# First feed-forward block: slices run on across batches two apart, time mixing's sums, keys and running maximum one slice later

## The reference

```python
x = x + tanh(g_ffn[0]) * L0_ffn(layernorm(x))
#   up = x @ wu.T; gate = x @ wg.T; out = (silu(up) * gate) @ wd.T     wu, wg: 2048 x 512, ternary
x = x + tanh(g_xattn[1]) * L1_xattn(w, u, k=layernorm(x), v=ctx_2048)
#   time mixing, for t in 0..255, per channel, carrying (p, q, o):
#   no = max(o, u + k_t); A = exp(o - no); E = exp(u + k_t - no)
#   y_t = (A * p + E * v_t) / (A * q + E)
#   no2 = max(w + o, k_t); p, q = exp(w + o - no2) * (p, q) + exp(k_t - no2) * (v_t, 1)
```

## Time and profile before

| | us |
|---|---|
| median of three runs | 3331.32 (3331.31 to 3336.03) |
| profiled execution | 3330.52 |
| its span | 3328.7 |
| PE busy | 2915.2 (88%) |
| DVE busy | 2454.5 (74%) |
| ACT busy | 1777.8 (53%) |
| POOL busy | 939.5 (28%) |
| mean granted TensorE clock | 0.95 of full |

### The profile page before, as it was taken

How to read it: one execution, slowest core, us unless ns; L and a number is a source line. 1 busy time by engine, 2 the same in 40 slices (tenths; PEclk the granted TensorE clock), 3 DMA queues, 4 the chain that set the end, 5 groups by cost and what they waited for, 6 DMA issues and landing times.

```text
span 3328.7 us, 48608 instructions
## 1 busy us (share of the span) xinstructions
PE 2915.2 (88%) x18346; PEld 1700.8 (51%) x18346; DVE 2454.5 (74%) x4452; ACT 1777.8 (53%) x2803; POOL 939.5 (28%) x1409
## 2 busy tenths in 40 slices
PE   8999989883899898668888667999999999998999
PEld 4444766652444444456666433545455445443666
DVE  7887578887666666788888668777777777776433
ACT  3331455555455554089998964444454444445444
POOL 5543000002200000046776774222222222211000
PEclk9999999996899999889999878999999999999999
DMA  7422212212111011100000021000000000011000
GB/s 251 142 98 74 64 56 66 64 51 83 31 27 33 18 26 64 48 26 1 1 1 1 28 87 47 7 1 7 1 7 7 1 7 7 1 48 58 13 14 26
DMA packets 60422, 132.78 MB, mean 40 GB/s; under 512 B 6496, under 2 KB 27808, under 8 KB 59424
## 3 DMA queue, kind: packets, MB, share of 16 engines
q1 hardware_dynamic: 50976, 96.11, 9.3%
q10 hardware_dynamic: 9216, 33.56, 3.3%
HBM read 119.03 MB, written 4.19 MB: 37 GB/s over the span
## 4 chain that ended last, share of the span: by engine, by line
PE 46%; DVE 16%; ACT 9%; issue 4%; POOL 3%; DMA 0%; DVEq 0%; ACTq 0%; SPq 0%; POOLq 0%
PE psum L1289 10%; PE psum L2257 5%; PE psum L2787 4%; PE psum L3258 3%; PE psum L3236 3%; PE psum L2746 3%; ACT area_g L2332 3%; PE psum L2771 3%; PE psum L2138 2%; PE psum L2756 2%; PE psum L2278 2%; DVE area_a L1898 2%; PE psum L1544 2%; PE psum L1525 2%; ACT xn L2898 1%
## 5 line engine op out<-in xcount | busy, mean ns | idle before, releaser
L2332 ACT ACTIVATE area_g<-area_a 128x2048 bf16<-128x2048 f32 x168 | 334.6, 1995 | 31.6 <-POOL area_a L2201 22.4
L2257 PE MATMUL psum<-area_c,ident_bf 128*128 128x128 bf16 x3328 | 234.3, 236 | 94.1 <-DVE area_c L2366 94.0
L660 PE MATMUL psum<-area_b,area_g 128*128 128x512 f32 x640 | 280.9, 596 | 2.2 <-issue 2.2
L2257 PEld LDWEIGHTS psum<-area_c,ident_bf 128*128 128x128 bf16 x3328 | 219.0, 107 | 119.9 <-DVE area_c L2366 112.7
L2746 PE MATMUL psum<-area_b,stage 128*128 128x512 f32 (+1 forms) x512 | 237.5, 546 | 0.0
L848 PE MATMUL psum<-xT_high,area_a 128*128 128x256 f16 x1024 | 230.9, 276 | 4.4 <-DVE area_b L1095 2.9
L848 PE MATMUL psum<-xT_low,area_a 128*128 128x256 f16 x1024 | 230.5, 276 | 0.0
L2898 ACT ACTIVATE xn<-psum,small 128x384 f32<-128x384 f32 (+1 forms) x256 | 163.8, 640 | 96.0 <-DVE small L3037 95.8
L3037 DVE TENSOR_REDUCE small<-psum 128x1 f32<-128x384 f32 (+1 forms) x256 | 158.1, 618 | 71.5 <-PE psum L2747 69.0
L2663 POOL TENSOR_TENSOR small<-small,half_pow 128x4 f32<-128x4 f32 x96 | 131.8, 1373 | 273.6 <-DVE small L2984 273.6
L660 PEld LDWEIGHTS psum<-area_b,area_g 128*128 128x128 f32 x640 | 120.7, 191 | 148.2 <-issue 144.1
(11 more groups left out here) (426 smaller groups left out, 7388.7 us busy)
## 6 DMA issues: line engine op xcount, KB each, us to landing
stage<-in_w ACTq DMA_DIRECT2D x24, 512.0 KB, 4.5
stage<-in_w SPq DMA_DIRECT2D x24, 512.0 KB, 3.7
area_g<-in_toeplitz SPq DMA_DIRECT2D x32, 256.0 KB, 2.7
area_b<-in_ctxT SPq DMA_DIRECT2D x15, 512.0 KB, 4.1
area_b<-area_b SPq DMA_DIRECT2D x24, 256.0 KB, 3.7
stage<-in_ctxT SPq DMA_DIRECT2D x9, 512.0 KB, 3.8
x_stream<-in_x SPq DMA_DIRECT2D x4, 1024.0 KB, 8.0
area_c<-in_ctxT SPq DMA_DIRECT2D x8, 512.0 KB, 7.8
```

What stands on the lines that cost most here:

```text
L660: last = nc.tensor.matmul(psum[:, bank + m, :], toep[:, h % 2, (m - k) * P:(m - k + 1) * P], kv[:, h % 2, k, :], start=(k == 0), stop=(k = ...
L2257: last = nc.tensor.matmul(psum[:, 1, t_ * P:(t_ + 1) * P], identb[:, :], above5[:, t_, c * P:(c + 1) * P], start=(c == 0), stop=(c == KE - 1))
L2332: nc.scalar.activation(junk5[t_], z5[b % 3][:, t_, :], ACT.Sign, bias=fine5[:, par, t_:t_ + 1], scale=-1.0, accum_out=signs5[:, t_:t_ + 1] ...
```

## The change

TensorE: the last two downs of a batch move behind `up_gate` 0 and 1 of the next batch, so that `down` runs two slices behind `up_gate` throughout, and `y_back` of tile 0 goes with them; `keys` move from slices 2 and 3 to 3 and 4. ScalarE: `scaled` of time mixing moves from slice 0 to 1, `key_copy` from 2 and 3 to 3 and 4. VectorE: the addition to X becomes a function, `ffn0_add`, and goes from the end of the batch to slice 1 of the next one, behind L1115; time mixing's norm sums go from slice 0, ahead of L1115, to slice 1, behind `ffn0_add`; `running_max` goes from slice 4 to 5. The wait for `front_bank_free` is written inside the loop but stands where it stood. No instruction is added or dropped; POOL's and SP's orders stay.

```diff
@@ -866,9 +866,9 @@
             for t_ in range(TT):
                 transpose_front(pe, front_of_ffn(0), t_)
             for b in range(B):
-                f = front_of_ffn(b)
-                pe.wait_ge(sig("front_bank_free"), tile_no(f, TT))
                 for j in range(NJ):
+                    if j == 0:
+                        pe.wait_ge(sig("front_bank_free"), tile_no(front_of_ffn(b), TT))
                     if b == 0 and j < 2:
                         pe.wait_ge(sig("conv_added"), B + 3 + 2 * j)
                     if b == 0 and j == 2:
@@ -876,15 +876,19 @@
                     up_gate(b, j)
                     if j == 2:
                         y_back(b - 3, 1)
-                    if j in (2, 3):
-                        keys(b - 1, j - 2)
+                    if j in (3, 4):
+                        keys(b - 1, j - 3)
                     if j in (4, 6) and b + 1 < B:
                         transpose_front(pe, front_of_ffn(b + 1), j // 2 - 2)
                     if j >= 2:
                         down(b, j - 2)
-                down(b, NJ - 2)
-                y_back(b - 2, 0)
-                down(b, NJ - 1)
+                    elif b:
+                        down(b - 1, NJ - 2 + j)
+                    if j == 0:
+                        y_back(b - 3, 0)
+            down(B - 1, NJ - 2)
+            y_back(B - 3, 0)
+            down(B - 1, NJ - 1)
             keys(B - 1, 0)
             y_back(B - 3, 1)
             keys(B - 1, 1)
@@ -956,12 +960,12 @@
                                          ACT.Copy, scale=2.0 ** -26).then_inc(sig("hid_high_ready"), 1)
                     if j == 0:
                         present_exp(b - 2)
-                    if j == 0 and b:
+                    if j == 1 and b:
                         scaled(act, front_of_wkv(b - 1), b - 1)
                     if j == 3 and b + 1 < B:
                         scaled(act, front_of_ffn(b + 1), b + 1)
-                    if j in (2, 3):
-                        key_copy(b - 1, j - 2)
+                    if j in (3, 4):
+                        key_copy(b - 1, j - 3)
                     if j in (1, 2, 3, 5, 6):
                         sum_later(act, 5 * b + (1, 2, 3, 5, 6).index(j))
                     if j in (4, 6) and b + 1 < B:
@@ -1085,6 +1089,13 @@
                     nc.vector.tensor_tensor_scan(wk_p[:, k, 1:S + 1], wk_d[:, 2, k, :], wk_ev[:, k, :], 0.0,
                                                  ALU.mult, ALU.add).then_inc(sig("wkv_pq_ready"), 1)
 
+            def ffn0_add(b):
+                for t_ in range(TT):
+                    xt = X[:, b * TT + t_, :]
+                    dve.wait_ge(sig("down_ready"), b * TT + t_ + 1)
+                    nc.vector.scalar_tensor_tensor(out=xt, in0=psum[:, 6 + t_, :], scalar=S1("ffn0"), in1=xt,
+                                                   op0=ALU.mult, op1=ALU.add).then_inc(sig("ffn0_added"), 1)
+
             for b in range(B):
                 for j in range(NJ):
                     n = b * NJ + j
@@ -1094,16 +1105,13 @@
                                                            in1=psum[:, 2 + 2 * (j % 2), :], op0=ALU.add, op1=ALU.mult))
                     nc.vector.tensor_tensor(hid[:, j % 2, :], act_a[:, j % 2, :], psum[:, 3 + 2 * (j % 2), :],
                                             ALU.mult).then_inc(sig("hid_ready"), 1)
-                    if j == 0 and b:
-                        dve.wait_ge(sig("ffn0_added"), TT * b + TT)
-                        norm_sums(dve, dc, front_of_wkv(b - 1), b - 1)
                     if j == 1:
                         products(b - 2)
                     if j == 2:
                         totals(b - 2)
                     if j == 3:
                         invert(b - 2, 0)
-                    if j == 4:
+                    if j == 5:
                         running_max(b - 1)
                     if j in (5, 7) and b + 1 < B:
                         ffn_low(dve, (b + 1) * TT + (j - 5) // 2 + 1, (b + 1) % 2, (j - 5) // 2)
@@ -1116,6 +1124,10 @@
                                                    in0=hid[:, j % 2, :].rearrange("p (m s) -> p m s", m=2),
                                                    scalar=2.0 ** -26, in1=hTh[:, 2 * j:2 * j + 2, :], op0=ALU.mult,
                                                    op1=ALU.subtract).then_inc(sig("hid_low_ready"), 1)
+                    if j == 1 and b:
+                        ffn0_add(b - 1)
+                        dve.wait_ge(sig("ffn0_added"), TT * b + TT)
+                        norm_sums(dve, dc, front_of_wkv(b - 1), b - 1)
                     if j in (0, 3):
                         add_y(b - 3, j // 3)
                     if j == 2 and b + 1 < B:
@@ -1125,12 +1137,8 @@
                     if j == 7:
                         weights_scan(b - 1)
                 values_scan(b - 1)
-                for t_ in range(TT):
-                    xt = X[:, b * TT + t_, :]
-                    dve.wait_ge(sig("down_ready"), b * TT + t_ + 1)
-                    nc.vector.scalar_tensor_tensor(out=xt, in0=psum[:, 6 + t_, :], scalar=S1("ffn0"), in1=xt,
-                                                   op0=ALU.mult, op1=ALU.add).then_inc(sig("ffn0_added"), 1)
             c = B - 1
+            ffn0_add(c)
             dve.wait_ge(sig("ffn0_added"), TT * B + TT)
             norm_sums(dve, dc, front_of_wkv(c), c)
             products(c - 1)
```

## The result

| | before | after |
|---|---|---|
| median of four runs, us | 3331.89 | 3393.92 (3384.72 to 3397.35) |
| ratio | 1 | 1.0189, 95% interval 1.0177 to 1.0201 |
| profiled execution (its span) | 3330.52 (3328.7) | 3390.84 (3389.1) |

The change costs 62 us; 3397 was forecast. ScalarE's tanh is now L956, its key copy L910, `ffn0_add` L1096.

A forecast was written before the change was run, and what follows sets the result against it. Neither TensorE nor VectorE is full; waits set the batch. Redone links sum to 61.27 us a batch against 52.21, +53.4 over the block, plus 12.0 for the clock: 3395.9 profiled, median 3397, range 3377 to 3416.

The forecast's parts named there:

- S(0) of batch 0 to S(7) of batch 7: Block between starts of VectorE's first instruction in those slices: +53.4 us at full clock, +65.4 with clock loss.
- Slice 1 to 2: Link between VectorE's slice starts: 5.34 us becomes 13.46, as ScalarE's tanh of slice 2 queues behind `scaled`.
- The 4.22 us: Term of slice 1 to 2: from the norm sums' end to VectorE's next slice start, now with nothing covering it.
- Slice 4 to 5: Link between VectorE's slice starts: 4.56 us becomes 8.53, as keys' and front transposes meet in PSUM bank 0.
- the clock: TensorE's lower clock after the slice 4 wait: 2.0 us a batch, bounds 0 and 3.2, 12.0 over batches 1 to 6.
- TensorE's wait for `ffn0_add`: At a new batch's first down group: about 3.6 us idle, not on the path.
- A: Rival: TensorE no longer drains, its waits and their clock loss go, 41 us less: 3290 us; faster 0.05, same 0.03.
- B: Rival: one of the two links is hidden; if the front transposes' wait, 36 us fall away: 3361 us; chance 0.07.
- C: Rival: clock stays at 1.2 GHz through the slice 4 link, costing 5.7 us, not 2.0: +22 us, 3419; chance 0.10.

The follow-up runs named there:

- experiment 1: Changed kernel with ScalarE's `scaled` of time mixing in slice 2 in place of slice 1: 3375.6 us, 1.0138.
- experiment 3: Changed kernel with `scaled` in slice 2 and the next batch's front transposes and `ffn_high` in slices 5 and 6: 3343.0 us, 1.0044.
- experiment 2: Changed kernel with the next batch's front transposes and `ffn_high` in slices 5 and 6 in place of 4 and 6: 3365.5 us, 1.0111.
- experiment 4: Kernel before with only `keys` and `key_copy` moved to slices 3 and 4 and `running_max` to slice 5: 3370.0 us, 1.0124.
- experiment 10: Kernel of experiment 3 with tanh of the next slice ahead of ScalarE's other steps in slices 0 to 3: 3338.8 us, 1.0033.
- experiment 9: Kernel before with tanh of the next slice ahead of ScalarE's other steps in slices 0 to 3 only: 3311.6 us, 0.9952.
- experiment 8: Kernel of experiment 1 with VectorE's `totals` at the end of slice 2, behind the norm sums: 3361.0 us, a single run.
- experiment 11: Changed kernel with `ffn0_add` and the norm sums ahead of the products in slice 1: 3386.0 us, 1.0174.

## Why the prediction was right

**Size and place.** In the profiled runs, S(0) of batch 0 to S(7) of batch 7 went from 393.25 to 457.54 us: +64.3, forecast +65.4. The block started 1.6 us earlier (the first stages varied by up to 3.3 us from run to run, changed or not) and 2.3 us came back behind it: 60.4 in the span. The block is within 1.1 us of the forecast. That the median came within 3 us as well is partly luck: the rest of the program alone varied by 12 us between traces.

**Slice 1 to 2** was right in kind and within 0.15 us. The 4.22 us that I took from before held 0.28 of POOL's L777 (0.48 beside VectorE's L1115 then, 0.20 now); VectorE's own part of the slice was 0.14 longer than summed, which hid half of that. Experiments 1 and 3 show the queue order as its cause.

**Slice 4 to 5** was right: shown from both sides by experiments 2 and 4. Over the six batches it came to 63.6 us; 6 x 8.53 = 51.2 at full clock leaves 12.4 for the clock, where 12.0 stood in the sum. The loss came every batch, 1.5 to 2.7 us, inside the bounds of 0 and 3.2. In batches 4 and 5 the bank was free 2.69 us after S(4) (2.55 forecast), and from there TensorE took 7.42 and 8.55 us against 5.98 in the sum, at a granted clock of 0.72 and 0.64: four transposes took 1.08 us in place of 0.60, the down group 2.95 and 3.62 in place of 1.90. So the clock's part is shown, but its size, 2.0, was met partly by luck. It was what whole batches lost in clock before, and little of that reached the path: with the same wait of 2.90 us, the slice 4 link was 4.45 us in batch 2, where the clock stayed at 1.00, and 4.56, 4.56, 5.66 and 4.56 in batches 3 to 6, where it did not. It happened to fit a link of which more than half passes at the lower level.

**Waits off the path.** TensorE's wait for `ffn0_add` was 1.7 to 4.3 us, 3.6 forecast. It is shorter where the clock after the preceding 2.94 us wait was low and TensorE arrived later, and the link of VectorE did not move: it is off the path.

**Rivals.** A failed: with tanh of slice 2 freed and the two transposes apart (experiment 3) the run-on still is no gain, and experiment 10 against 9 puts it 27 us behind. What these two compare is the run-on together with sums, keys and running maximum one slice later; the run-on without those was not run. B failed, both links were whole. C failed: 2.1 us a batch, not 5.7.

**What stays open.** How much of the 27 us between experiments 9 and 10 is the held POOL and how much the keys' later place was not tried. The 2.9 us by which slice 1 to 3 is longer (13.9 against 11.0) are neither: VectorE has no wait there in batch 5, and does the additions to X and the norm sums that it did elsewhere before; slices 7 to 0 and 0 to 1 are 2.0 shorter for it.

## What to carry to other kernels

A step moved one slice later on one engine takes its place in a queue: look at what is queued behind the instruction that will wait, and at who shares the PSUM bank in the slice it moves to. Adding up the links between one engine's marks, each redone with the new orders, gave the block's 64 us to about 1; the stalls of TensorE that look largest are not those links. Where a short instruction that everyone needs (tanh) can stand ahead of one that waits for a round over two engines, put it there, but not across a point where its own input comes late.

## What the runs showed of the hardware

VectorE held up GpSimd, which the forecast had nothing of: a 128x1 instruction took 2.40 us beside two 128x1024 f32 additions with both inputs in SBUF, and 0.27 elsewhere. Beside instructions with one input in PSUM (L1104, L1106) GpSimd was not held: in experiment 8 L777 and L778 took 0.20 and 0.70 us there, as they do beside an idle VectorE in the changed kernel. The Trainium skill, "SBUF — State Buffer", section "Who interferes with whom", says that a VectorE instruction with two SBUF inputs contends with a GpSimd instruction that reads SBUF; experiments 1, 8 and 11 agree. In experiments 8 and 11 POOL got in between two of VectorE's long instructions (1.01 us, then 1.55 or 1.56); in experiment 1 the hold spanned both. What makes the difference was not tried.
